# Ranges of 16 nodes, own edges written with the zeros, basis merges and the root split moved in a two-layer graph network

## What is computed

```
xw  = x @ W.T
h   = segment_sum(dinv[row]*dinv[col] * xw[row], col)   # + loop edges, + b
h   = gelu(batch_norm(h)) + x
x   = layernorm(x + h)
# then twice, with basis1.. and basis2..:
w    = einsum('rb,bio->rio', att, basis)                # 30 bases of 512x512, R = 2
msg  = where(type == 0, g0*x_j @ w[0], g1*x_j @ w[1])   # g = sigmoid(x_j @ gate_w)
agg  = segment_sum(msg, row) + x @ root + bias          # relu after the first
out = layernorm(x + agg)
```

## Time and profile before

| | us |
|---|---|
| median of 3 runs | 328.7 (328.42 to 328.86) |
| profiled execution, device time | 328.01 |
| its span, first to last instruction | 326.2 |
| PE busy | 291.7 (89%) |
| DVE busy | 179.9 (55%) |
| ACT busy | 140.9 (43%) |
| POOL busy | 48.1 (15%) |
| moved by DMA | 73.66 MB, 226 GB/s over the span |
| chain that ended last: PE, DVE, DMA, issue | 69%, 16%, 5%, 5% |

### The profile page before, as it was taken

How to read it: one execution, slowest core, us unless ns; L and a number is a source line. 1 busy time by engine, 2 the same in 40 slices (tenths; PEclk the granted TensorE clock), 3 DMA queues, 4 the chain that set the end, 5 groups by cost and what they waited for, 6 DMA issues and landing times.

```text
span 326.2 us, 4834 instructions
## 1 busy us (share of the span) xinstructions
PE 291.7 (89%) x1709; PEld 198.1 (61%) x1709; DVE 179.9 (55%) x502; ACT 140.9 (43%) x274; POOL 48.1 (15%) x80
## 2 busy tenths in 40 slices
PE   0778999997898999647999999999997999999991
PEld 0644656643336668414686655657796877787771
DVE  3789987999979755688401024035246125433333
ACT  5499997989710458748225213220412242100000
POOL 2334400000000920372000000000001900010000
PEclk9999999999796799969999999999999999999997
DMA  6972888599797799909999578979000510001112
GB/s 174 341 318 96 332 330 291 245 395 420 293 393 304 257 317 409 401 36 335 418 353 406 194 280 337 378 280 363 13 0 0 132 31 0 2 0 32 31 33 63
DMA packets 12757, 73.66 MB, mean 226 GB/s; under 512 B 1952, under 2 KB 2195, under 8 KB 4540
## 3 DMA queue, kind: packets, MB, share of 16 engines
q1 hardware_dynamic: 11282, 70.82, 57.1%
q0 software_dynamic: 1104, 2.36, 2.9%
q10 hardware_dynamic: 346, 0.17, 0.2%
HBM read 72.05 MB, written 1.28 MB: 225 GB/s over the span
## 4 chain that ended last, share of the span: by engine, by line
PE 69%; DVE 16%; DMA 5%; issue 5%; ACT 1%; POOL 1%; DVEq 1%; SPq 0%; POOLq 0%
PE psW L490 13%; PE psM L471 11%; PE psM L473 10%; PE psM L472 10%; PE psM L712 7%; PE psM L732 6%; PE psE L566 5%; DVE oh_key L1050 4%; PE psM L618 3%; DMA basis_ring<-in_L_gnn_basis_dram 3%; DMA xs<-in_x_dram 3%; DVE w L1033 1%; DVE B L1040 1%; DVE x_sum L1167 1%; DVE AT L1100 1%
## 5 line engine op out<-in xcount | busy, mean ns | idle before, releaser
L490 PE MATMUL psW<-basis_ring,S 128*32 128x512 f32 x512 | 65.9, 634 | 1.0 <-DMA basis_ring<-in_L_gnn_basis_dram 1.0
L1050 DVE TENSOR_SCALAR oh_key<-iota_f,key 128x320 f16<-128x320 f16 x162 | 46.8, 330 | 4.9 <-DVE B L1040 1.7
L1214 DVE SCALAR_TENSOR_TENSOR zg<-psM,gate,zg 125x512 fp32r<-125x512 f32 x20 | 15.0, 751 | 57.9 <-ACT zg L904 57.9
L566 PE MATMUL psE<-oh_key,oh_src 128*125 128x320 f16 x162 | 35.6, 340 | 5.5 <-DVEq L1042 3.7
L566 PEld LDWEIGHTS psE<-oh_key,oh_src 128*125 128x125 f16 x162 | 21.9, 145 | 25.2 <-issue 13.9
L780 ACT ACTIVATE oh_diff<-iota_f,edgeT 128x128 f16<-128x128 f16 x108 | 34.3, 389 | 1.5 <-ACT xT_full L794 0.8
L904 ACT ACTIVATE zg<-psM,gate 125x512 fp32r<-125x512 f32 x20 | 13.8, 689 | 46.1 <-PE psM L473 45.7
L471 PE MATMUL psM<-w,hlT 128*125 128x512 f32 x80 | 32.4, 405 | 0.1
L490 PEld LDWEIGHTS psW<-basis_ring,S 128*32 128x32 f32 x512 | 13.7, 113 | 29.8 <-issue 26.1
L473 PE MATMUL psM<-w,hlT 128*125 128x512 f32 x80 | 31.6, 395 | 0.0
L472 PE MATMUL psM<-w,hlT 128*125 128x512 f32 x80 | 31.6, 395 | 0.0
(11 more groups left out here) (161 smaller groups left out, 451.3 us busy)
## 6 DMA issues: line engine op xcount, KB each, us to landing
basis_ring<-in_L_gnn_basis_dram SPq DMA_DIRECT2D x64, 1024.0 KB, 6.8
root_raw<-in_L_gnn_root_dram POOLq DMA_DIRECT2D x32, 64.0 KB, 3.5
xs<-in_x_dram SPq DMA_DIRECT2D x1, 1120.0 KB
out_dram<-xs SPq DMA_DIRECT2D x5, 224.0 KB
w_raw<-in_L_gnn_W_dram SPq DMA_DIRECT2D x1, 1024.0 KB, 10.4
bias_b<-in_L_gnn_bias_dram POOLq DMA_DIRECT2D x1, 250.0 KB, 3.3
xs<-in_x_dram SPq DMA_DIRECT2D x1, 130.0 KB
out_dram<-xs SPq DMA_DIRECT2D x5, 26.0 KB
```

The lines of the kernel that those rows point to most:

```text
L490: m = nc.tensor.matmul(psW[32 * j:32 * j + 32, cc % 2, :], S[:, cc % 2, cc // CH, q].rearrange("p k r -> p (k r)"), ring[:, n % RING, j, : ...
L566: nc.tensor.matmul(psE[0:PC, g % 2, 0:KEYS], oh_src[:, g % 3, j * P:j * P + PC], oh_key[:, t % OH, :], start=(j == 0), stop=(j == G - 1)). ...
L1050: v.tensor_scalar(oh_key[:, t % OH, :], iota_f[:, 0:KEYS], key[:, t:t + 1], None, ALU.is_equal) \
L1214: link(v.scalar_tensor_tensor(out=zg[:, 1, c, r, :], in0=bank(("Z", L, c, r))[0:PC, :], scalar=gate[:, L, c, r:r + 1], in1=zg[:, 0, c, r, ...
```

## The change

Everything is moved or resized; what is computed stays the same.

- W is 16 and a range is 3 tiles (SG), so there are NW = 54 windows of 160 columns, two for each group of 6 tiles. Both windows of a group share a bank. DVE adds them behind tiles 1 and 3 of a group, and `add_window` waits for the one before instead of for itself.
- The turned inputs lose their full copy and POOL's part: ACT makes the high part, DVE subtracts straight from the bank (`turned_low`), nine steps at the ends of groups 1 to 5. The turns move behind the base matmul.
- ACT writes the identity into B behind the zeros; L1102 goes.
- `w_merge(2)` moves behind z. POOL makes `diag`, ahead of its 16 DMAs. The spreading of dinv comes behind the first half aggregate on PE, and ACT copies it out.
- root1's high part is made by ACT behind block f = 0 of the aggregates, its low part by POOL behind each inverse root; they lie in other memory (root1_lo in w block 3), so `w_high(3)` waits for the end of x @ root1.
- `w_merge(3)` moves from the layer norm to behind the third `x1_lo`; `w_low(3)`, `w_merge(4)`, `w_high(4)`, `w_low(4)`, `w_first(5)`, `w_merge(5)`, `w_high(5)`, `w_first(6)` and `w_low(5)` each move one or two places later; pair 22 moves from x @ root1 to behind the first Z block.
- W0 is loaded in four DMAs with its rows in another order, and vecT is kept once.

The diff, cut to what the prediction speaks of (declarations, shapes and the twin lines of the window sizes are left out):

```diff
-W = 32
+SG = 3
+NW = T // SG
+W = 16
...
+                if (f, h) == (0, 0):
+                    for i in range(2):
+                        use(("dinv", i), "act")
...
+        FIRST_TURNS = 3
+        TURN_AT = {0: (3,), 1: (4, 5), 2: (6, 7), 3: (8,)}
+        TURNED_LOW_AT = {1: (0, 1), 2: (2, 3), 3: (4, 5), 4: (6, 7), 5: (8,)}
...
 
             pool.wait_ge(deg_ready, 1)
             nc.gpsimd.tensor_tensor(dinv_p[:], deg[:], mhalf[0:PC, 0:NC], ALU.pow).then_inc(dinv_ready, 1)
+            pool.wait_ge(dinv_ready, 1)
+            for c in range(NC):
+                nc.gpsimd.tensor_scalar(diag[:, c, :], ident[0:PC, 0:PC], dinv_p[:, c:c + 1], None, ALU.mult) \
+                    .then_inc(diag_ready, 1)
...
+            def root1_low(k):
+
+                pool.wait_ge(root_hi, k + 1)
+                nc.gpsimd.tensor_tensor(in_q(root1_lo[:, k]), natural(root1_raw[:, k]), in_q(root1_hi[:, k].bitcast(F32)),
+                                        ALU.subtract).then_inc(root_ready, 1)
...
-            for k in range(KC - 1):
-                root1_low(k)
+                root1_low(f)
...
+                    at = j // SG * KEYS
+                    nc.tensor.matmul(psE[0:PC, g % 2, at:at + KEYS], oh_src[:, g % 3, j * P:j * P + PC],
+                                     oh_key[:, t % OH, :], start=(j % SG == 0), stop=(j % SG == SG - 1)) \
+                        .then_inc(adj_used, 1)
+                for i in TURN_AT.get(g, ()):
+                    turn(i)
...
+                    if (f, h) == (0, 0):
+                        pe.wait_ge(diag_ready, NC)
+                        for i, (c0, c1) in enumerate(((0, 4), (4, NC))):
+                            wait_free(pe, ("dinv", i))
+                            for c in range(c0, c1):
+                                last[0] = nc.tensor.matmul(bank(("dinv", i))[:, (c - c0) * PC:(c - c0 + 1) * PC],
+                                                           ones_f[0:PC, :], diag[:, c, :], start=True, stop=True)
+                            done()
...
                         x1_turned(EARLY + f)
-                    basis_upto(39 + KC * h + f)
+                    basis_upto(min(39 + KC * h + f, 43))
...
                         if L == 0:
-                            basis_upto(47 + 7 * (R * c + r) // 5)
+                            basis_upto((45, 47, 49, 51, 51, 53, 55, 55, 57, 59)[R * c + r])
...
-                if pp == WBLK - 2:
-                    act.wait_ge(adj_used, T)
+                if pp in (3, WBLK - 2):
+                    act.wait_ge(main_full, uses[("root1", KC - 1, 1)] + 1)
...
+            link(nc.scalar.activation(counts, ones_f[0:PC, 0:1].broadcast_to(list(counts.shape)), ACT.Copy, scale=0.0))
+            for c in range(NC):
+                nc.scalar.activation(B[:, c, 0, c * PC:(c + 1) * PC], ident[0:PC, 0:PC], ACT.Copy).then_inc(b_zero, 1)
+            def turned_high(i):
+                wait_full(act, turned[i])
+                hi, _, ps = turned_parts(i)
+                nc.scalar.activation(hi, ps, ACT.Copy).then_inc(in_hi, 1)
...
+            for i, (c0, c1) in enumerate(((0, 4), (4, NC))):
+                wait_full(act, ("dinv", i))
+                link(nc.scalar.activation(dinv_b[:, c0 * PC:c1 * PC], bank(("dinv", i))[:, 0:(c1 - c0) * PC], ACT.Copy))
+                act.sem_inc(free_act, 1)
+                act.sem_inc(dinv_b_ready, 1)
...
                             ("bb", b), "act")
+                if f == 0:
+                    act.wait_ge(root1_in, 16 * KC * JB)
+                    for k in range(KC):
+                        nc.scalar.activation(in_q(root1_hi[:, k]), natural(root1_raw[:, k]), ACT.Copy).then_inc(root_hi, 1)
...
                     nc.scalar.activation(hf[:, f - 1, :], hf[:, f - 1, :], ACT.Gelu, bias=bn[:, 1, f - 1:f],
                                          scale=bn[:, 0, f - 1:f]).then_inc(gelu_done, 1)
-            act.wait_ge(root1_in, 16 * KC * JB)
-            act.wait_ge(main_full, uses[("agg0", KC - 1, 1)] + 1)
-            for k in range(KC):
-                nc.scalar.activation(in_q(root1_hi[:, k]), natural(root1_raw[:, k]), ACT.Copy).then_inc(root_hi, 1)
...
-            w_high(3)
             w_first(4)
...
-                    if (h, f) == (1, 1):
-                        w_high(4)
-                        w_first(5)
+            w_high(3)
...
-                    if L == 0 and c == 2:
+                    if L == 0 and c == 0:
+                        w_high(4)
+                        w_first(5)
+                    if L == 0 and c == 3:
                         w_high(5)
...
+            def turned_low(i):
+
+                dve.wait_ge(in_hi, i + 1)
+                hi, lo, ps = turned_parts(i)
+                link(v.tensor_tensor(lo, ps, hi.bitcast(F32), ALU.subtract))
+                dve.sem_inc(free_dve, 1)
+                dve.sem_inc(in_lo, 1)
...
                 dve.wait_ge(basis_used, SUB * (2 * pp + 2))
                 dve.wait_ge(w_hi, R * pp)
+                dve.wait_ge(w_lo, R * pp)
...
+            def add_window(w):
+
+                g, h = w // 2, w % 2
+                at = nc.values_load(base_i[0:1, w:w + 1], engines=[mybir.EngineType.DVE], min_val=0, max_val=N - 1)
+                if h == 0:
+                    dve.wait_ge(adj_used, G * (g + 1))
+                if w:
+                    dve.wait_ge(win_added, w)
...
+                v.tensor_tensor(to, to, psE[0:PC, g % 2, h * KEYS:(h + 1) * KEYS]
+                                .rearrange("p (c t w) -> p c t w", c=NC, t=R), ALU.add).then_inc(win_added, 1)
...
+                if t == G - 1:
+                    v.tensor_copy(base_i[:], gmm[0:1, 0, :])
...
+                if t % G == G - 1:
+                    for i in TURNED_LOW_AT.get(t // G, ()):
+                        turned_low(i)
+                if t == ROUNDS_AT * G:
...
+                if t % G in (1, 3) and t > 2 * G:
+                    add_window(t // SG - 4)
...
-                link(v.tensor_tensor(AT[:, c], B[:, c, 0, 0:N2], B[:, c, 1, 0:N2], ALU.add))
-                d = AT[:, c, c * PC:(c + 1) * PC]
-                v.tensor_tensor(d, d.bitcast(F32), ident[0:PC, 0:PC], ALU.add).then_inc(at_ready, 1)
-            w_merge(2)
+                v.tensor_tensor(AT[:, c], B[:, c, 0, 0:N2], B[:, c, 1, 0:N2], ALU.add).then_inc(at_ready, 1)
...
+            w_merge(2)
+            dve.wait_ge(dinv_b_ready, 2)
...
                 variance(c)
-                if c == 1:
-                    w_merge(3)
...
             for c in range(EARLY):
                 x1_lo(c)
-            w_low(3)
+            w_merge(3)
             for c in range(EARLY, NC):
                 x1_lo(c)
...
+            w_low(3)
             w_merge(4)
-            w_low(4)
...
-                    if L == 0 and c == 1:
+                    if L == 0 and c == 0:
+                        w_low(4)
+                    if L == 0 and c == 2:
                         w_merge(5)
-                    if L == 0 and c == 3:
+                    if L == 0 and c == 4:
                         w_low(5)
...
 
+            for d in range(NC):
+                own_edge = BB[:, d * (R * NC + 1) * PC:(d * (R * NC + 1) + 1) * PC]
+                last = v.tensor_tensor(own_edge, own_edge.bitcast(F32), ident[0:PC, 0:PC], ALU.subtract)
+            link(last)
```

More of the change, by code:

```diff
@@ L255, in gnn_block @@
         use("deg", "dve")
-        for h in range(2):
-            use(("dinv", h), "dve")
         NBB = -(-NC * R * NC // 4)
@@ L556, in _ @@
             done()
[L557 removed]
+            for i in range(FIRST_TURNS):
                 turn(i)
```

177 lines of the change are left out of this document (61 added, 116 removed).

## The result

The change makes the kernel slower: 352.49 us median of 4 runs (348.48 to 354.65) against 328.78 (328.42 to 330.5) on the same chip, ratio 1.0669 [1.0624, 1.0714]. Medians are over all executions, ratios leave out the slow ones (354.65 here, 351.03 of e2, 354.10 of e9). The prediction was 341.5, range 332 to 348: the sign and the four places where PE stands were right; the gain in the edge loop and the cost of the early root1 split were not. The profiled execution of the change is its fastest (348.48, span 346.7), so it shows 20.5 us of the loss; e13's profile (354.06, span 352.2) shows 26. Both have to be explained.

The account below looks back on a forecast made before the run. The prediction took PE as the bound from 110 us on wherever its operands are there, so waits put into its queue are paid. Its terms summed to +13.5 on the profiled 328.0, giving 341.5 us, range 332 to 348 (8 in 10).

Parts of the forecast that it names:

- the four places where PE stands: PE waits ahead of the second BB block of f = 1, pair 18, the first Z block and pair 26.
- Edge loop: Loop over edge groups: smaller windows and keys outweigh nine low parts on DVE; -5.8 us, 1.5 ahead of the loop included.
- AT to dinv: Between loop and dinv: identity additions and own waits go, degrees are copied sooner; -2.6 us.
- Spreading behind the first aggregate: Behind z on PE: the 2.19 us of spreading now follow the first half aggregate in PE's queue; +2.1 us.
- root1 early: Ahead of the second BB block of f = 1: PE stands while ACT awaits root1's DMAs; +5.6 us, clock +2.2.
- w_merge(3): Behind the third x1_lo: the merge delays pair 18, x @ root1 starts 1.6 later, clock 2.2; +3.8 us.
- w_high(3) late +1.3, w_first(6) +0.5: PE waits for w_lo at the first Z block, +1.3 us; ACT's copies come late behind Z (3, 1), +0.5.
- w_merge(5): Behind Z (2, 1): pair 26 waits on PE for the merge one block late; +4.2 us, clock +2.2.
- That the clock stays up: Rival: PE's stands of 5.6, 4 and 4.2 us do not lower its clock; 334.9 us, 17%.
- That register loads decide the loop: Rival: DVE's register loads make an edge-loop group 2.4 us instead of 2.05; 346.0 us, 12%.
- That POOL and DVE block each other: Rival: POOL's diag and root1 low parts hold z's low parts and the batch norm steps; 344.6 us, 10%.
- The stream as pace of PE: Rival: basis chunks pace PE from 110 us on, waits come back, only early gains stay; 319.6 us, 9%.

Follow-up runs that it names:

- e2: Changed kernel with w_merge(3) on VectorE inside the layer norm again; 3.3 us less than the changed kernel by the medians.
- e9: Changed kernel with diag on VectorE and the spreading ahead of the first aggregate again, root1 still early; 1.6 us less by the medians.
- e13: The changed kernel itself, unchanged, run again for a second profile; 353.08 us against 329.16 for the kernel before, ratio 1.0702.
- e7: e4 with the nine low parts of the turned inputs on GpSimd again, behind ScalarE's full copies; 2.6 us less than e4 by the medians.
- e3: Changed kernel with root1's high parts behind the last Gelu and low parts behind the inverse roots again; 12.7 us less than the changed kernel.
- e12: Changed kernel with the moves of e1, e2 and e3 undone at once; 24.4 us less than the changed kernel.
- e8: e4 with w_merge(2) behind z's low parts, as in the change; 325.06 us against 325.79.
- e1: Changed kernel with w_merge(5) on VectorE behind Z (1, 1) again; 6.2 us less than the changed kernel.
- e5: Changed kernel with idle matmuls in PE's queue at three stands (second BB block of f = 1, pairs 18 and 26); 4.2 us less.
- e6: Changed kernel with GpSimd's four root1 low parts behind all four inverse roots, high parts still early; 3 us slower by the medians.
- e14: Changed kernel with root1's high parts on ScalarE behind the first Gelu (f = 1); 343.33 us against 353.08.
- e4: Kernel before with only the change's part up to the node degrees, all later work as before; 3 us faster than before by the medians.
- e10: e7 and e8 together, all later work placed as in the kernel before; 2.4% faster than the kernel before.
- e11: e10 with 29 idle matmuls where PE rests; 2.3 us slower than e10 by the medians.

## Why the prediction was right in sign and 7 to 11 us short

Two terms were far off: the edge loop won 4.4 us less than forecast, and the early root1 split cost 3.0 to 5.9 more. The others were right within 1 us, the clock behind the stands among them.

**Edge loop, forecast -5.8, measured -1.4 (wrong).** The step that failed is "DVE pays nine low parts ... which lie in groups 1 to 5, where it had stood behind POOL": the stands are taken as free time, and no row says how long they were. In the kernel before seven of POOL's nine subtractions held a VectorE step, two ahead of the loop (the earlier trace rows show one) and five key steps in it, by 0.7 to 1.0 us each, 4.6 in all (timeline of DVE of before; such a step is 0.29 otherwise):
```profile
17.71 1.31 DVE L1050 TENSOR_SCALAR oh_key<-iota_f,key 128x320 f16<-128x320 f16 x1
```
Nine low parts at 0.93 are 8.3 in exchange, 1.86 for a group with two. Beside them stands the idle time ahead of windows that no releaser explains: 2.5 us between the windows at 22.42 and 41.53 of the change, none between 24.70 and 40.27 of before, 0.45 in the same groups of e7. Windows came every 4.45 us in groups 3 to 5 of the change, every 2.25 to 3.2 before. At group 14 DVE was 1.8 late and not 4.4 early. Behind it the steady group was better than forecast (1.82, not 2.05), and 36.2 us became 33.0, in spite of basis waits of 1.85 and 1.43 that the forecast had at 0.3. A second, small error: PE's six matmuls were taken at 0.95 from start to start where the trace before has 0.76. e7 puts this term back: with the low parts on POOL the last window is at 91.7. It does so for both causes at once; they are not separated.

**AT to dinv, -2.6 forecast, -3.3 measured (6.2 for 9.5).** Right, slightly better.

**Spreading behind the first aggregate, +2.1.** e3 and e12, which keep it without the early root1, have 30.6 from dinv to Gelu against 28.8: +1.8. It is there from the first aggregate of f = 1 on, which starts 11.7 behind dinv in both, 9.9 in the kernel before and 10.0 in e8, where only w_merge(2) is moved. Right. The diag pieces were 0.72 each and not 0.3 to 0.45, which put the root1 issues 1.7 later than forecast; e9, which takes them away, cannot tell what this was worth.

**root1 early, +5.6 and clock +2.2, measured 10.8 and 13.7 (mis-sized).** The place and the mechanism (bank order, ACT at the wait for root1) were right, and in the fastest execution the stand (5.58) and the longest landing (5.4) too. Two steps failed. First, the landing, "4.6 to 6.9 us, median 5.9": one execution was taken for all. The longest was 5.4, 7.8, 7.8 and 13.9 us, and the stand 5.6, 9.1, 9.15 and 12.8 (change, e13, e1, e9). Of the 3.5 between the change and e13 the landing makes 2.3; the other 1.2 is PE, which in the change comes to the wait later, since its clock was down (PE alone, columns as in the earlier trace rows; e13 has 1.00 from 109 to 111):
```profile
108.00:110.00 2.00, 2.00 (x12) 0.50 0.93 381
```
Second, the sum had nothing for the batch norm steps held by GpSimd, which stood only in a rival: 1.9 (0.80 and 1.38 where 0.14 is usual). So the change's 10.8 are 5.6 of stand, 1.7 for pair 14 at half clock, 1.9 held and 1.2 for the clock ahead of it; e13's 13.7 are 9.1, 1.7, 1.9 and 0.6 for an aggregate at half clock behind pair 14. About 0.4 is left in each.

**What the landing goes by is not settled.** The longest is the last of the 16 in the change, e13, e8 and e9, and the last to land in every run. Where it was issued behind both basis chunks of a pair, within 1.6 us, it took 7.2 to 9.0 us (e1, e3, e5, e6, e12, e13, e14); between the two, 5.4 (the change, e2). That fits the spread between executions, and no run sets this order on purpose. It does not cover the runs that issue earlier: e8 and e9, with both chunks just behind, took 13.5 and 13.9, and e4, e7, e10 and e11 6.6 to 9.3.

**w_merge(3), +3.8; measured 4.1 (e2, e12).** Right. Of it 2.2 were the clock, and e5 has 2.5.

**w_high(3) late +1.3, w_first(6) +0.5.** PE waits 1.36 at the first Z block and 0.18 at pair 28; e12 has 1.8 for both against e4. Right in the sum.

**w_merge(5), +4.2 and clock +2.2.** A stand of 4.66 and 1.3 on the pair, 5.8 to 6.2 by e1. Right.

**Rivals.** That the clock stays up is refuted (e5 has to be helped to it). That register loads decide the loop: the idle time ahead of windows that no releaser explains is 5.7 us over 54 windows, but the steady group is 1.82 long; refuted as the bound behind group 14, while ahead of it this time is a real cost (2.5 us up to the window at 41.53). That POOL and DVE block each other is half right: root1's low parts hold the batch norm (1.9, the rival said 1.5), diag does not hold z's low parts for long (3.73 for five in place of 3.39). The rule of the Trainium skill ("SBUF — State Buffer", "Who interferes with whom"), two SBUF inputs on DVE against a GpSimd instruction that reads SBUF, agrees with e6 and not with z beside diag: z's step reads two SBUF tiles, GpSimd's one, and they ran side by side, at 0.85 a step in place of 0.74. The held step of the earlier trace rows has one SBUF tile as input, and the rule says nothing of it. The stream as pace of PE is refuted for the part behind 110 us (e1 won all of its stand), and shows as waits of 1.85 and 1.43 in the last third of the loop.

Forecast errors: loop 4.4, AT -0.7, root1 3.0 and, against e13, 2.9 more at root1 and 2.0 for an e13 in which dinv is later; the others cancel within 1.

## What to carry to other kernels

A transfer's landing time read from one execution is no bound for a queue that will wait for it: take the slowest of the batch over several executions, look at what else is issued beside the last one, and put the wait where the engine has other work. A moved operation costs its full length on its new engine unless the row shows that engine idle there for the same reason after the change. Before a move to GpSimd, look which VectorE steps it will lie beside: each of a chain of small ones can be held for a whole GpSimd instruction, as in e6.

## What the runs showed of the hardware that was not expected

- The last of 16 DMAs of 64 KB landed after 5.4 us in one execution of the change and after 7.8 in another, and after 13.5 and 13.9 in e8 and e9, which issue it about 4 us sooner. At the end of the longest the 16 DMA engines were busy only 10% of the time (e9), as much as 1.6 of them would be.
- Three 1-column VectorE steps beside four GpSimd subtractions took 1.38, 1.44 and 1.44 us: after each GpSimd instruction VectorE got one step in, and then waited for the next.
- GpSimd's product of a 125x125 tile with a column took 0.72 us and made the VectorE steps beside it 0.11 us longer, no more; its 128x512 subtraction took 1.26 on natural order (before) and 1.51 on permuted (root1).
- Idle matmuls kept PE's clock up over stands of 4 to 6 us (e5), and in another kernel the same means was followed by a fall of the clock where there had been none (e11).
